# A graph network on one core: in the attention's second pass, odd chunks are weighted on POOL and even chunks on DVE

## The chip, the cores and the metric

The kernel runs on one core of a Trainium2 chip. The metric is the device time of one execution in microseconds (us). A core has several engines that run side by side, each with its own in-order list of instructions: PE (TensorE, matrix products into PSUM), DVE (VectorE, elementwise work), ACT (ScalarE, functions), POOL (GpSimd, slower elementwise work and indirect gathers) and SP, which here only issues DMA transfers. They hand work to each other through semaphores: an instruction adds to one when it is done, and another engine waits for a value.

## The reference

Four graph layers run one after the other over the same 3125 nodes (256 features) and 100000 edges, with a layer norm after each. The one that the change touches is the third, an attention over the edges that end in a node:

```
h = (x @ W.T).reshape(n, H, D)                      # H = 8 heads of D = 32
alpha = leaky(einsum(h[src], a_src) + einsum(h[dst], a_dst) + sum(enc * h[dst]))
amax = segment_max(alpha, dst)
ex = exp(alpha - amax[dst])
denom = segment_sum(ex, dst)
attn = ex / max(denom[dst], 1e-10)
out = segment_sum(h[src] * attn[..., None], dst)
return out.reshape(n, H * D) + bias
```

## The kernel before

The edges are sorted by the node in which they end and cut into NCD = 808 chunks of 128 edges, one edge for each of the 128 partitions. The nodes stand in 25 blocks of 128, and a chunk's edges all end in one block. The attention has two passes over the chunks. The first gathers the source rows h[src] (with POOL's indirect DMAs), makes the logits `alpha`, follows their maxima, and writes the gathered rows to `rows_spill` in DRAM. The second pass, which the change touches, turns them into sums. It starts with an all-engine meeting (`meet`), after which DVE carries the maxima from chunk to chunk (`carry_vector`, L1976 to L1997, some 70 us, with small products on PE at L1963), in two halves of 404 chunks; once a half's logits are lowered by their maxima, ACT may take their exponentials.

Then, for each chunk c, five engines work in a chain.

- SP reads the chunk's rows (128 x 256 values, 128 KB) from `rows_spill` into slot c % 16 of `hs` (L1921). It does so once the rows that the slot held, those of chunk c - 16, have been weighted.
- ACT, for each group of four chunks, writes the exponentials for the 8 heads into columns D to TW (256 to 263) of four of the eight slots of `msg` (L1951). It may do so once the chunk that used the last of these slots before has been summed by PE: for group i that is chunk 4i - 5. ACT also makes the one-hot matrices `oh3` that say in which row of its block each edge ends (L1942 and L1944, five instructions a group), seven groups deep.
- DVE multiplies each row by its exponentials, head by head, from `hs` into columns 0 to 255 of slot c % 8 of `msg` (`weighted_rows`, L1928). Both inputs lie in SBUF. It waits for the exponentials, for the rows, and for PE to have summed chunk c - 8.
- PE multiplies the one-hot matrix with the 264 columns of `msg` (L1973) into PSUM bank c % 8. In the profile this is two weight loads and two matmul records a chunk.
- DVE adds the bank to the sums of the chunk's block in `big` (L2012), four chunks behind its multiplication; one input is in PSUM, one in SBUF. The block's number is in a register. Sixteen of them are loaded at once (L82), so once in sixteen chunks. Consecutive chunks often have the same block, so each sum waits for the one before it to be complete (`added`).

Program order on DVE is thus: multiply chunk n, add chunk n - 4, multiply chunk n + 1, add chunk n - 3, and so on. POOL clears `hsrc` at the start of the pass (L1933) and then waits for the meeting that ends it.

The semaphores are used again under other names, and the rows of the program show the first name: `prefix_kept` is `msgs_v` (messages made by DVE), `mids_g` becomes `msgs_g`, `blocks_counted` is `exps`, `lanes_turned` is `accs_zeroed`.

Of the kernel before, what the change touches and what calls it, by code (L numbers as in the profile page):

```python
# [9 lines left out]
def up(n, m):  # L10
    return -(-n // m) * m
# [17 lines left out]
NCD = up((E + (P - 1) * NB) // P, 8)  # L29
GS = 2  # L30
NUS = up((E + (GS * P - 1) * NB) // (GS * P), 16)
# [54 lines left out]
def program(nc, t, out):  # L86
    with ExitStack() as ctx:
        v, a, pe, g, sp = nc.vector, nc.scalar, nc.tensor, nc.gpsimd, nc.sync
        known = {}

        def signal(name):
            if name not in known:
                known[name] = Signal(ctx.enter_context(nc.semaphore(name)))
            return known[name]

        def again(old, count):

            new = Signal(old.s)
            new.over(old.base + count)
            return new  # L100
# [52 lines left out]
        def lanes(col, n, k):  # L153
            return col.rearrange("p (n o) -> p n o", o=1).to_broadcast([col.shape[0], n, k])
# [1162 lines left out]
        mixed, mids_v, mids_g = signal("mixed"), signal("mids_v"), signal("mids_g")  # L1317
# [381 lines left out]
        RB = 16  # L1699
# [214 lines left out]
        carry_used, lowered = again(counted_used, 2), again(counted_hot, 2 * NBATCH)  # L1914
        exps, msgs_v = again(step_done, NBATCH + 1), again(prefix_kept, NBATCH)

        def sums_sync():
            for c in range(NCD):
                if c >= RB:
                    sp.wait_ge(msgs_v.s, msgs_v.n(c - RB + 1))  # L1920
                sp.dma_start(hs[:, c % RB, :], rows_spill[c]).then_inc(spill.s(c, RB), 16)  # L1921

        def weighted_rows(eng, c):
            eng.wait_ge(exps.s, exps.n(c // 4 + 1))
            eng.wait_ge(spill.s(c, RB), spill.n(c, RB))
            if c >= 8:
                eng.wait_ge(summed.s, summed.n(c - 7))
            return eng.tensor_tensor(msg[:, c % 8, 0:D].rearrange("p (h d) -> p h d", h=H),  # L1928
                                     hs[:, c % RB, :].rearrange("p (h d) -> p h d", h=H),
                                     lanes(msg[:, c % 8, D:TW], H, HD), ALU.mult)  # L1930

        def sums_pool():
            g.memset(hsrc, 0.0).then_inc(accs_zeroed.s, 1)  # L1933

        def sums_scalar():
            for n in range(NCD + 6):
                if n < NCD and n % 4 == 0:
                    i, hot = n // 4, oh3[n // 4 % OH3]
                    if i >= OH3:
                        a.wait_ge(summed.s, summed.n(4 * (i - OH3) + 4))  # L1940
                    for k in range(4):
                        ins = a.activation(hot[:, k, :], iota, ACT.Abs, bias=recd3[:, n + k, D_DL:D_DL + 1], scale=-1.0)  # L1942
                    then_a(ins)
                    a.activation(hot, hot, ACT.Relu, bias=1.0, scale=-1.0).then_inc(hot_made.s, 1)  # L1944
                c = n - 6
                if c >= 0 and c % 4 == 3:
                    i = c // 4
                    a.wait_ge(lowered.s, lowered.n(1 if 4 * i + 4 <= CH else 2))
                    if i >= 2:
                        a.wait_ge(summed.s, summed.n(4 * i - 4))  # L1950
                    a.activation(msg[:, 4 * (i % 2):4 * (i % 2) + 4, D:TW], alpha[:, 4 * i:4 * i + 4, :],  # L1951
                                 ACT.Exp).then_inc(exps.s, 1)

        def sums_tensor():
            pe.wait_ge(carried.s, carried.n(1))
            k = 0
            for half in range(2):
                cs = slice(half * CH, (half + 1) * CH)
                for h in range(H):
                    for reach in (fwd, bwd):  # L1960
                        if k >= 8:
                            pe.wait_ge(carry_used.s, carry_used.n(k - 7))
                        pe.matmul(ps[k % 8][:, 0:CH], lanes(ident[0:H, h:h + 1], 1, P)[:, 0, :], reach[:, cs],  # L1963
                                  start=True, stop=True).then_inc(carry_spread.s, 1)
                        k += 1
            pe.wait_ge(carry_used.s, carry_used.n(4 * H))
            pe.wait_ge(accs_zeroed.s, accs_zeroed.n(1))
            for c in range(NCD):
                pe.wait_ge(hot_made.s, hot_made.n(c // 4 + 1))
                pe.wait_ge(msgs_v.s, msgs_v.n(c + 1))  # L1970
                if c >= 8:
                    pe.wait_ge(added.s, added.n(c - 7))
                pe.matmul(ps[c % 8][:, 0:TW], oh3[c // 4 % OH3][:, c % 4, :], msg[:, c % 8, :],  # L1973
                          start=True, stop=True).then_inc(summed.s, 1)
# [24 lines left out]
        def sums_vector():  # L1999
            blk = Numbers(v, regs_v, blk_d_row, NB - 1)  # L2000
            v.wait_ge(accs_zeroed.s, accs_zeroed.n(1))
            for n in range(NCD + 4):
                c = n
                if c < NCD:
                    weighted_rows(v, c).then_inc(msgs_v.s, 1)
                c = n - 4
                if c >= 0:
                    v.wait_ge(summed.s, summed.n(c + 1))
                    if c >= 1:
                        v.wait_ge(added.s, added.n(c))  # L2010
                    here = big[:, bass.ds(blk.at(c) * TW, TW)]
                    v.tensor_tensor(here, here, ps[c % 8][:, 0:TW], ALU.add).then_inc(added.s, 1)  # L2012
            v.wait_ge(added.s, added.n(NCD))

        sums_sync()
        sums_pool()
        sums_scalar()
        sums_tensor()
        carry_vector()
        sums_vector()  # L2020
        summed.over(NCD)
        added.over(NCD)
# [134 lines left out]
```

## Time and profile before

| | |
|---|---|
| median of 3 runs | 10667.19 us |
| lowest, highest | 10627.23, 10682.18 us |
| the profiled execution | 10687.69 us |
| its span | 10685.9 us |
| second pass, first weighted row to last sum | 8720.1 to 9329.3 us |
| DVE, PE, ACT busy in 8720 to 9330 | 553.07, 545.84, 400.20 us |
| POOL busy in 8720 to 9330 | 0.00 us |

The span runs from the first instruction to the last. A timeline row gives the start, the duration, the engine, the line and the operands, and in square brackets how long the engine had been idle and what released it. On DVE, instructions overlap a little: a multiplication is recorded with 0.42 us, but the next instruction may start 0.34 us after it. So what a sequence costs is read from the starts, not from the durations.

### The profile page before, as it was taken

Reading aid. Unit: us, or ns where it says so; the run is one execution under the profiler, and the core shown is the slowest. Engines: PE = TensorE matmul, PEld = TensorE weight load, DVE = VectorE, ACT = ScalarE, POOL = GpSimd, SP = SyncE. Lnnn points to the kernel's source line nnn. Section 1 sums busy time; section 2 is a strip of 40 time slices with the busy share of each in tenths; the row PEclk is TensorE's granted clock in tenths of the full one; section 3 lists DMA queues with packets and bytes.
Section 4 is the critical chain, followed back from the end, with each engine's and each line's share of the span. In section 5 each row is a group of like instructions: output and inputs, shape, how many; then the busy total and the mean of one; then the engine's idle time right before and its main releaser. Section 6 shows DMA issues by size and latency. Waiting matters only on the chain. (4 is left out here: it accounts for less than half of the span.)

```text
span 10685.9 us, 108870 instructions
## 1 busy us (share of the span) xinstructions
PE 6312.3 (59%) x23693; PEld 3434.3 (32%) x23693; DVE 5953.1 (56%) x17820; ACT 2842.7 (27%) x9327; POOL 5768.1 (54%) x6086
## 2 busy tenths in 40 slices
PE   2211344446865666666667777765555578856665
PEld 1101233334433333433334111233333333333332
DVE  8915533430016666544445999976656589943333
ACT  0000000105862222100003777762222236500000
POOL 5776566561006666566662888844555510046664
PEclk9999855558987877888887999996666679978877
DMA  2000111113553333433332555534666645523333
GB/s 79 6 6 5 36 42 46 44 33 124 176 194 96 93 93 93 109 91 91 91 90 67 168 171 169 171 91 141 189 184 186 185 128 176 153 80 91 92 91 82
DMA packets 782920, 1136.72 MB, mean 106 GB/s; under 512 B 161213, under 2 KB 631923, under 8 KB 775629
## 3 DMA queue, kind: packets, MB, share of 16 engines
q0 software_dynamic: 246400, 552.44, 19.6%
q1 hardware_dynamic: 535885, 577.31, 16.6%
q8 instruction: 216, 3.54, 0.1%
q14 instruction: 419, 3.43, 0.1%
HBM read 872.21 MB, written 257.00 MB: 106 GB/s over the span
## 5 line engine op out<-in xcount | busy, mean ns | idle before, releaser
L1155 POOL DMA_INDIRECT ring<-scaled_table,idx_s x832 | 787.2, 946 | 1181.1 <-DVEq L192 773.7
L1029 POOL DMA_INDIRECT big<-x_table,rec_d_sb x808 | 806.1, 998 | 1101.1 <-DMA x_table<-big 726.0
L1748 POOL DMA_INDIRECT ring<-att_table,rec_d_sb x808 | 775.6, 960 | 750.7 <-DVE acc L1858 287.6
L1427 PE MATMUL bank<-ring,wts 128*128 128x512 f32 x1664 | 937.6, 648 | 397.2 <-issue 166.7
L1105 PE MATMUL bank<-iota 128*128 128x512 bf16 x2448 | 1090.0, 445 | 0.0
L333 POOL DMA_INDIRECT rec_s<-acc,big x784 | 837.6, 1068 | 375.0 <-issue 253.7
L1349 POOL DMA_INDIRECT ring<-y_table,idx_s x832 | 815.2, 980 | 395.5 <-DVEq L192 171.3
L333 POOL DMA_INDIRECT rec_d<-x_res,big x784 | 750.5, 957 | 502.0 <-DVE big L596 255.5
L1155 POOL DMA_INDIRECT ring<-h_table,rec_d_sb x808 | 764.1, 946 | 470.6 <-issue 180.4
L1116 PE MATMUL bank<-big,ring 128*128 128x256 f32 x1616 | 620.5, 473 | 501.0 <-issue 363.7
L2088 PE MATMUL bank<-ring 128*128 128x256 f32 x1664 | 644.9, 475 | 421.0 <-DVE ring L2070 244.4
L1182 PE MATMUL bank<-ring 128*128 128x256 f32 x1616 | 634.5, 480 | 387.0 <-issue 354.8
L1370 ACT ACTIVATE ring<-ring,big 128x64 f32<-128x64 f32 x2496 | 680.3, 335 | 269.1 <-DVE ring L1392 171.8
L1767 PE MATMUL bank<-big 128*128 x2424 | 622.8, 388 | 198.7 <-issue 129.6
L1174 DVE TENSOR_TENSOR acc<-acc,bank 128x256 f32 x808 | 340.4, 421 | 622.6 <-PE bank L1182 257.1
L400 ACT COPY big<-bank 128x425 f32<-128x425 f32 x49 | 25.2, 514 | 2195.6 <-PE bank L455 1613.6
L1116 PEld LDWEIGHTS bank<-big,ring 128*128 128x128 f32 x1616 | 375.7, 242 | 718.6 <-issue 640.1
L1427 PEld LDWEIGHTS bank<-ring,wts 128*128 128x128 f32 x1664 | 253.8, 191 | 1080.4 <-issue 472.6
L1973 PE MATMUL bank<-ring 128*128 128x264 f32 x1616 | 545.8, 425 | 78.5 <-issue 58.6
L1855 DVE TENSOR_TENSOR ring<-bank,wts 128x256 f32<-128x256 f32 x808 | 337.6, 418 | 440.9 <-ACT wts L1809 257.1
L2088 PEld LDWEIGHTS bank<-ring 128*128 128x128 f32 x1664 | 328.7, 223 | 761.9 <-DVE ring L2070 434.4
L1809 ACT ACTIVATE wts<-bank 128x256 f32<-128x256 f32 x808 | 302.1, 383 | 998.5 <-remote 453.6
(344 smaller groups left out, 13324.4 us busy)
## 6 DMA issues: line engine op xcount, KB each, us to landing
weights_dram<-acc SPq DMA_DIRECT2D x104, 1024.0 KB, 4.5
ring<-weights_dram SPq DMA_DIRECT2D x832, 128.0 KB
rows_spill<-ring SPq DMA_DIRECT2D x808, 128.0 KB
big<-rows_spill SPq DMA_DIRECT2D x808, 128.0 KB, 2.2
ring<-key_dram SPq DMA_DIRECT2D x49, 1024.0 KB
big<-dl_dram SPq DMA_DIRECT2D x50, 512.0 KB
ring<-y_table,idx_s POOLq DMA_INDIRECT x832
ring<-scaled_table,idx_s POOLq DMA_INDIRECT x832
```

The costliest lines, as they stand in the source:

```text
L333: g.indirect_dma_start(out=table, out_offset=bass.IndirectOffsetOnAxis(ap=row_of[k][:, j:j + 1], axis=0), in_=stage[:, j, :], in_offset=No ...
L1029: g.indirect_dma_start(out=xg[:, c % RG, :], out_offset=None, in_=x_table, in_offset=bass.IndirectOffsetOnAxis(ap=recd3i[:, c, D_IDX:D_IDX ...
L1105: pe.matmul(ps[7].rearrange("p (o k) -> p o k", o=2), iota[:, 0:P // 2].bitcast(BF16), spare, start=True, stop=True)
L1116: pe.matmul(ps[c % 7][:, 0:D], onehot[:, c % 8, :], xg[:, c % RG, 0:D], start=True, stop=True).then_inc(summed.s, 1)
L1155: g.indirect_dma_start(out=slot[:, c % ring_len, :], out_offset=None, in_=table, in_offset=bass.IndirectOffsetOnAxis(ap=index(c), axis=0)) ...
L1182: pe.matmul(ps[c % 7][:, 0:D], hot4[:, c % 4, :], hg[:, c % R2, :], start=True, stop=True).then_inc(summed.s, 1)
L1349: g.indirect_dma_start(out=yg[:, n % RY, MUL:], out_offset=None, in_=y_table, in_offset=bass.IndirectOffsetOnAxis(ap=idx_s[:, n:n + 1], ax ...
L1370: ins = a.mul(dots[:, c % 2, d * MUL:(d + 1) * MUL], y[:, (1 + d) * MUL:(2 + d) * MUL], recs3[:, c, S_SH + 1 + d:S_SH + 2 + d])
L1427: pe.matmul(ps[6 + u % 2], oh1[c // 4 % 2][:, c % 4, :], mid[:, c % 2, 0:512], start=(c % GS == 0), stop=(c % GS == GS - 1)).then_inc(summ ...
L1748: g.indirect_dma_start(out=ag[:, n % R3, :], out_offset=None, in_=att_table, in_offset=bass.IndirectOffsetOnAxis(ap=recd3i[:, n, D_IDX:D_I ...
L1767: ins = pe.matmul(ps[c % 3][:, 0:TW], hot_n[:, i % 3, k * P:(k + 1) * P], big_b[:, bass.ds(at + s * TW, TW)], start=(s == 0), stop=(s == 2))
L2088: pe.matmul(ps[3 + u % 4][:, 0:D], oh4[:, c % 4, :], sg[:, c % R4, :], start=(c % GS == 0), stop=(c % GS == GS - 1)).then_inc(summed.s, 1)
```

## The change

POOL multiplies the rows of the odd chunks, 404 of the 808, in a list of its own after it has cleared `hsrc`; DVE multiplies those of the even chunks. The function is the same, with another engine. The messages are counted by two semaphores, one for each engine, and those who wait for a message (PE, before the product, and SP, before it reads new rows into the slot) wait for the one that belongs to the chunk. DVE still adds every chunk, at the same place.

```diff
+        msgs_g = again(mids_g, NUS)
+
+        def message_made(eng, c):
+
+            made_by = msgs_g if c % 2 else msgs_v
+            eng.wait_ge(made_by.s, made_by.n(c // 2 + 1))
+
         def sums_sync():
             for c in range(NCD):
                 if c >= RB:
-                    sp.wait_ge(msgs_v.s, msgs_v.n(c - RB + 1))
+                    message_made(sp, c - RB)
...
         def sums_pool():
             g.memset(hsrc, 0.0).then_inc(accs_zeroed.s, 1)
+            for c in range(1, NCD, 2):
+                weighted_rows(g, c).then_inc(msgs_g.s, 1)
...
-                pe.wait_ge(msgs_v.s, msgs_v.n(c + 1))
+                message_made(pe, c)
...
-                if c < NCD:
+                if c < NCD and c % 2 == 0:
                     weighted_rows(v, c).then_inc(msgs_v.s, 1)
```

On DVE, this stands in a row before, from the multiplication of chunk 8 to that of chunk 11 (L1928 multiplies, L83 sets the register with the block's place, L2012 adds):

```order
L1928 TENSOR_TENSOR ring<-big,ring 128x256 [waits summed,spill8,blocks_counted]
L83 ISA [waits added,summed]
L2012 TENSOR_TENSOR big<-big,bank4 128x264
L1928 TENSOR_TENSOR ring<-big,ring 128x256 [waits summed,spill9,blocks_counted]
L83 ISA [waits added,summed]
L2012 TENSOR_TENSOR big<-big,bank5 128x264
L1928 TENSOR_TENSOR ring<-big,ring 128x256 [waits summed,spill10,blocks_counted]
L83 ISA [waits added,summed]
L2012 TENSOR_TENSOR big<-big,bank6 128x264
L1928 TENSOR_TENSOR ring<-big,ring 128x256 [waits summed,spill11,blocks_counted]
```

And with the change, from the same chunk 8 on (L1935 multiplies, L2021 adds):

```order
L1935 TENSOR_TENSOR ring<-big,ring 128x256 [waits summed,spill8,blocks_counted]
L83 ISA [waits added,summed]
L2021 TENSOR_TENSOR big<-big,bank4 128x264
L83 ISA [waits added,summed]
L2021 TENSOR_TENSOR big<-big,bank5 128x264
L1935 TENSOR_TENSOR ring<-big,ring 128x256 [waits summed,spill10,blocks_counted]
L83 ISA [waits added,summed]
L2021 TENSOR_TENSOR big<-big,bank6 128x264
L83 ISA [waits added,summed]
L2021 TENSOR_TENSOR big<-big,bank7 128x264
L1935 TENSOR_TENSOR ring<-big,ring 128x256 [waits summed,spill12,blocks_counted]
```

Every second addition now follows directly on the one before it. On POOL, the odd chunks' multiplications follow the clearing of `hsrc`:

```order
L1940 MEMSET big 128x6600 [waits engines_met]
L1935 TENSOR_TENSOR ring<-big,ring 128x256 [waits spill1,blocks_counted]
L1935 TENSOR_TENSOR ring<-big,ring 128x256 [waits spill3,blocks_counted]
L1935 TENSOR_TENSOR ring<-big,ring 128x256 [waits spill5,blocks_counted]
L1935 TENSOR_TENSOR ring<-big,ring 128x256 [waits spill7,blocks_counted]
L1935 TENSOR_TENSOR ring<-big,ring 128x256 [waits summed,spill9,blocks_counted]
L1935 TENSOR_TENSOR ring<-big,ring 128x256 [waits summed,spill11,blocks_counted]
```

Before, nothing stood behind the MEMSET on this engine until the meeting; now 404 multiplications do, each of which waits for its exponentials, its rows and, from chunk 9 on, for PE.

## Rows read from the trace of the kernel before

**Rows 1.** Busy time by stretch: start:end, length, engines, clock share, DMA, GB/s
```profile
8646.00:8720.00 74.00, 46.33 (x64) 19.73 (x64) 69.64 (x72) 10.88 (x31) 5.60 (x1) 0.50 0.09 29
8720.00:9330.00 610.00, 545.84 (x1616) 242.54 (x1616) 553.07 (x1619) 400.20 (x1185) 0.00 (x0) 1.00 0.58 171
```

**Rows 2.** Timeline, DVE in the pass: start, duration, engine, line [idle before]
```profile
8998.23 0.42 DVE L1928 TENSOR_TENSOR ring<-big,ring 128x256 f32<-128x256 f32 x1
8999.66 0.43 DVE L2012 TENSOR_TENSOR big<-big,bank 128x264 f32 x1 [1.01 <-PE bank L1973]
9000.00 0.42 DVE L1928 TENSOR_TENSOR ring<-big,ring 128x256 f32<-128x256 f32 x1
9000.34 0.42 DVE L2012 TENSOR_TENSOR big<-big,bank 128x264 f32 x1
...
9011.57 0.43 DVE L2012 TENSOR_TENSOR big<-big,bank 128x264 f32 x1 [1.02 <-PE bank L1973]
```

**Rows 3.** Timeline, DVE at the pass's end, where additions follow additions
```profile
9326.32 0.42 DVE L2012 TENSOR_TENSOR big<-big,bank 128x264 f32 x1
9326.96 0.43 DVE L2012 TENSOR_TENSOR big<-big,bank 128x264 f32 x1 [0.22 <-DVE big L2012]
9327.61 0.43 DVE L2012 TENSOR_TENSOR big<-big,bank 128x264 f32 x1 [0.22 <-DVE big L2012]
```

**Rows 4.** Timeline, all engines at the pass's start
```profile
8720.11 1.76 DVE L1928 TENSOR_TENSOR ring<-big,ring 128x256 f32<-128x256 f32 x5
8720.67 3.42 PE L1973 MATMUL bank<-ring 128*128 128x264 f32 x7 [17.78 <-DVE ring L1928]
8723.18 0.43 DVE L2012 TENSOR_TENSOR big<-big,bank 128x264 f32 x1 [1.31 <-PE bank L1973]
```

**Rows 5.** Busy time by stretch, as rows 1: start of the pass; a later product
```profile
8720.60:8724.10 3.50, 3.42 (x8) 2.73 (x9) 2.19 (x7) 0.00 (x0) 0.00 (x0) 0.50 0.64 185
9410.30:9413.00 2.70, 2.70 (x14) 2.10 (x12) 2.27 (x6) 0.37 (x1) 0.00 (x0) 1.00 0.00 0
```

**Rows 6.** Timeline, PE in that later product
```profile
9410.31 2.75 PE L913 MATMUL bank<-wts,ring 128*128 128x256 f32 x12
```

**Rows 7.** Timeline, from chunk 19's multiplication to ACT's next exponentials
```profile
8732.98 0.41 DVE L1928 TENSOR_TENSOR ring<-big,ring 128x256 f32<-128x256 f32 x1
...
8733.46 0.30 PEld L1973 LDWEIGHTS bank<-ring 128*128 128x128 f32 x2 [0.38 <-issue]
...
8734.27 0.23 ACT L1951 ACTIVATE ring<-acc 128x32 f32<-128x32 f32 x1 [0.64 <-PE bank L1973]
...
8734.41 1.26 ACT L1942 ACTIVATE ring<-iota,rec_d_sb 128x128 f32<-128x128 f32 x4
8735.70 0.63 ACT L1944 ACTIVATE ring<-ring 128x512 f32<-128x512 f32 x1
```

**Rows 8.** Second layer, L1341 and its instructions: duration ns min/median/max, first and last start
```profile
L1341 POOL TENSOR_TENSOR ring<-ring,big x416: 507/517/694, 5808.1 to 7102.9; 128x192 f32<-128x192 f32 x139
```

**Rows 9.** Timeline, second layer, POOL and DVE, POOL released by DVE
```profile
6213.61 0.28 DVE L1400 TENSOR_TENSOR ring<-ring 128x128 f32<-128x128 f32 x1
...
6213.97 0.51 POOL L1341 TENSOR_TENSOR ring<-ring,big 128x192 f32<-128x192 f32 x1 [0.63 <-DVE ring L1400]
```

**Rows 10.** Timeline, second layer, POOL and DVE at once, inputs in SBUF
```profile
6501.59 0.36 DVE L1397 TENSOR_TENSOR ring<-ring 128x192 f32<-128x192 f32 x1 [0.18 <-PE bank L1427]
6501.63 0.68 POOL L1341 TENSOR_TENSOR ring<-ring,big 128x192 f32<-128x192 f32 x1
...
6501.86 0.60 DVE L1400 TENSOR_TENSOR ring<-ring 128x128 f32<-128x128 f32 x1
```

**Rows 11.** Timeline, second layer, POOL beside an addition from PSUM
```profile
6142.90 0.52 POOL L1341 TENSOR_TENSOR ring<-ring,big 128x192 f32<-128x192 f32 x1
6142.93 0.68 DVE L1414 TENSOR_TENSOR acc<-acc,bank 128x512 f32 x1
```

**Rows 12.** L1414 and its instructions in the whole second layer
```profile
L1414 DVE TENSOR_TENSOR acc<-acc,bank x416: 672/674/689, 5813.6 to 7104.8; 128x512 f32 x139
```

## The prediction

> **What bounds the kernel now.** I read the busy times by stretch first. In the second pass (8720 to 9330) DVE is busy 553 us of 610 and PE 546, while POOL has nothing and PE has its full clock, 1.00 [rows 1]. Busy time doesn't say which of DVE and PE is the bound, since both overlap their own instructions. The timeline of DVE does. A multiplication starts 0.34 us after an addition and an addition 0.34 us after a multiplication: 8999.66, 9000.00, 9000.34 [rows 2]. That is about 0.675 us for a chunk without a gap, and PE follows at that pace: its weight load starts 0.48 us after the multiplication [rows 7]. PE could go faster. Its records of 256 columns in a product without waits take 2.75 us for 12, 0.23 each, at clock 1.00 [rows 5, 6], so 0.24 for 264 columns and 0.47 for a chunk of two. ACT has five instructions and the exponentials in a group of four chunks, from 8734.27 to about 8736.33, 2.1 us out of 2.7 [rows 7]. So DVE is the bound.
>
> DVE also has a hole every sixteen chunks, when it loads block numbers: 8998.23 to 8999.66 is 1.43 us where 0.34 is usual, 1.09 too much, and the next such addition comes 11.91 us after this one [rows 2]. The name of PE in that row is misleading: PE is up to date there, and the distance is just that of L82's load of sixteen numbers. 11.91 is 16 times 0.676 and 1.09.
>
> **What leaves DVE, and what comes to light.** 404 multiplications leave it. At 0.34 us each that would be 136 us. But an addition must wait for the one before it, and the rows at the end of the pass show what that costs where nothing is between: 9326.32, 9326.96, 9327.61, a start every 0.65 us, with DVE idle 0.22 us and released by L2012 itself [rows 3]. Before, the multiplication filled just this hole: addition to addition with it takes 9000.34 less 8999.66, 0.68 us [rows 2]. Taking it out gives 0.65 in place of 0.675, and that is all. For two chunks DVE now has multiplication, addition, addition: 0.337 + 0.65 + 0.337 = 1.325 us in place of 1.35. The gain is 0.025 us for each of 404 pairs, 10.1 us. The load of the numbers stays, at the same place behind a multiplication of an even chunk.
>
> At the start, five multiplications stand before the first addition, 1.76 us in all [rows 4]; three stand there now, which is 0.7 us less, or nothing if PE, which runs at clock 0.50 there, 0.49 us a record [rows 4, 5], is late with its first sums. I take 0.7.
>
> **What POOL costs itself.** No row shows a 128 x 256 multiplication on POOL. The nearest is the same operation with 192 columns and a broadcast input, 517 ns [rows 8]. The bounds are 0.52 us (no dependence on the width) and 0.69 us (in proportion, 517 x 256 / 192). I take 0.66, nearer to the upper one, because 0.52 us for 192 columns must be mostly per element. POOL needs one in 1.325 us, so it is half idle at either bound, and its list has nothing else until the meeting. It starts within 0.08 us of its releaser: L1400 ends at 6213.89, POOL starts at 6213.97 [rows 9]. SP and PE wait for the same messages as before through another semaphore; I cost this at nothing, as POOL's come earlier than DVE's did.
>
> **Where POOL and DVE meet.** In the second layer a POOL multiplication that started at 6501.63 took 0.68 us instead of 0.52, behind a DVE multiplication that had started at 6501.59; and the DVE multiplication issued at 6501.86 took 0.60 us, where the same one takes 0.28 [rows 9, 10]. DVE thus worked from 6502.18 to 6502.46, and stood until 0.13 us before POOL's end. The two exclude one another while POOL reads: 0.52 less 0.13 is 0.39 us for 192 columns, and 0.66 less 0.13 is 0.53 us for 256. An addition with one input in PSUM isn't held: beside POOL from 6142.93 on it took 0.68 us [rows 11], and its median is 674 ns [rows 12]. So the 808 additions are free of it, the 404 multiplications left on DVE are not.
>
> The Trainium skill, "SBUF — State Buffer", section "Who interferes with whom", says that a DVE instruction with two SBUF inputs contends with a POOL instruction that reads SBUF, that the one that started first has the shared pair for its whole instruction and the other fully blocks, and that one SBUF input doesn't contend. The trace agrees, except that DVE was let in 0.13 us before POOL's recorded end. By the page's words alone the hold would be 0.66 instead of 0.53 us, which would put the hold's end below at 2.73 and cost 16 us in place of my 4.
>
> Does the hold fall on a multiplication? POOL's two instructions of a group both wait for the same exponentials, since the PE sum that frees their slots also frees ACT's. So they come as a pair each 2.65 us. Count from the start of the multiplication of chunk 4i-6 on DVE: PE starts after 0.48; it does that chunk and then chunk 4i-5, whose message is ready, 0.47 later; from a chunk's weight load to the exponentials it releases are 8734.27 less 8733.46, 0.81; exponentials 0.23; POOL 0.08 [rows 7, 9]. The sum is 2.07. POOL's first instruction then holds until 2.07 + 0.53 = 2.60. DVE's multiplications start at 1.325, 2.65 and 3.975. The one at 2.65 gets in by 0.05 us; POOL's second waits behind it until about 2.9 and holds until some 3.5, clear of 3.975. With 0.69 for POOL and 0.50 for PE's chunk the hold ends at 2.66, about 2 us over the 202 groups; with some tenths more it is slower in proportion, because DVE then waits in every group for a loop that starts with its own multiplication. I take 4 us, bounds 0 and 20, the latter for a loop that is 0.1 us longer.
>
> At the start, POOL's first four multiplications run during the carry stage, where the exponentials of the first half are ready; each can hold DVE by up to 0.53 us, 0 to 2.1. I take 1.
>
> **Sum.** -10.1 - 0.7 + 4 + 1 = -5.8 us. From the profiled execution's 10687.7 us that gives 10681.9. It stands 20.5 us above the median of the runs shown (10667.2), so on the median the forecast is 10661 us: no change that can be told, since a measurement of this kernel tells about 0.5%, 53 us.
>
> **Rivals.**
>
> Held multiplications (slower). If the loop is longer than I counted, POOL's first instruction of each pair takes hold just before DVE's multiplication. The most it can cost is the whole hold, 0.53 us in each of 202 groups, 107 us; if POOL's second also wins against the next multiplication, 404 x 0.53, 214 us. It decides by when POOL starts relative to 2.65: at 2.12 or before nothing is lost, from there on the loss grows by 0.1 us a group for each 0.1 us, and for a start past 2.65 DVE is first. For a result over 0.5% it needs 65 us of holds, 0.32 us a group, a loop of 2.97 instead of 2.65. For it: my margin is 0.05 us and four links were added up. Against it: 0.3 us is more than any one link seems off by. Typical time: 10667 - 11 + 107 = 10763. Chance 12%. Milder holds, 20 to 50 us net, stay within 0.5%; they have some 15% of the forecast's 81.
>
> The gain as meant (faster). If the 0.65 us between additions were not the wait for the one before but something that the multiplication on DVE costs too, all 0.337 x 404 = 136 us would go, down to 10531; PE's 0.47 and ACT's 2.1/4 a chunk would allow it. Rows 3 speak against it: there is no other work there, and the profile itself names L2012 as the releaser. 3%, with 2% for a median that scatter puts 0.5% lower.
>
> POOL as bound, or PE's clock lost (slower). POOL would need over 1.325 us for what takes 0.52 to 0.69, and PE's work is the same in slightly less time, so its clock of 1.00 has no reason to fall. At clock 0.50 a chunk costs 0.98 us [rows 4] against 11.91/16 = 0.744 [rows 2], 190 us more, 10857. 2%.
>
> **How the numbers follow.** No change to tell 81%, slower 14% (12 and 2), faster 5%. The likeliest case gives 10661. Its own scatter is that of the runs shown, 40 us down and 15 up from the median, and the milder holds add up to 50. The range 10620 to 10720 takes these in and leaves out the two far rivals.
>
> **What would show it.** In the changed kernel's timeline DVE should show multiplication, addition, addition with starts at 0.34, 0.65 and 0.34 us, and idle 0.22 before each odd addition, released by L2021. The pass should take about 600 us instead of 610, with DVE busy near 0.42 x 404 us less. POOL should show 404 instructions of 0.6 to 0.7 us, in pairs each 2.65 us, the second of a pair some 0.2 longer. Multiplications of 0.42 us on DVE mean that none is held; if every second one takes 0.6 to 0.9, the held rival is right, and the pass is longer than before. Additions closer than 0.6 us to one another would break the argument.

## The result, and the profile after

| | before | changed |
|---|---|---|
| median, 22 runs each | 10637.76 us | 10679.28 us |
| ratio, 95% interval | | 1.0036 [1.0018, 1.0053] |
| profiled execution's span | 10685.9 us | 10703.4 us |
| second pass, first row weighted by DVE to last sum | 8720.1 to 9329.3, 609.2 us | 8694.4 to 9354.3, 659.9 us |
| DVE's 404 multiplications of even chunks, mean | 416 ns | 572 ns |

The changed kernel is slower by 0.36%, 19 to 56 us. That is within the 0.5% that I had called no change, but it is clear of zero, and on the other side of the 6 us gain that I forecast. The spans of the two profiled executions hide most of it: the second pass began 26 us earlier in the changed one, in stages whose code is the same. The pass itself is 50.7 us longer, within the interval of the whole.

Three groups of the changed kernel in the pass; the columns are line, engine, operation, operands, count, then busy us and mean ns, then idle time before them and what ended it:

```profile
L2021 DVE TENSOR_TENSOR big<-big,bank 128x264 f32 x808 | 343.9, 426 | 145.6 <-DVE big L2021 87.1 <-PE bank L1982 57.6 <-issue 1.0
...
L1935 POOL TENSOR_TENSOR ring<-big,ring 128x256 f32<-128x256 f32 x400 | 238.6, 618 | 442.4 <-ACT ring L1960 442.4
L1935 DVE TENSOR_TENSOR ring<-big,ring 128x256 f32<-128x256 f32 x404 | 230.7, 572 | 0.4
```

The first line shows the hole that was to come to light: 87.1 us in which an addition waits for the one before it. Before, it was filled by multiplications, and such waits came to 0.9 us, as the same line of the kernel before shows:

```profile
L2012 DVE TENSOR_TENSOR big<-big,bank 128x264 f32 x808 | 339.6, 420 | 56.3 <-PE bank L1973 55.1 <-DVE big L2012 0.9 <-issue 0.3
```

The second line has 400 of POOL's 404 multiplications; the first four ran in the carry stage. The third line is the surprise: DVE's multiplications take 572 ns on average. At 0.418 us each, the duration of one that isn't held, 404 would take 169 us; they took 231. The 62 us more are what the pass lost, against 10 us won.

DVE at the start of the pass, in the timeline:

```profile
8711.97 0.42 DVE L1935 TENSOR_TENSOR ring<-big,ring 128x256 f32<-128x256 f32 x1
8712.30 0.42 DVE L2021 TENSOR_TENSOR big<-big,bank 128x264 f32 x1
8712.95 0.43 DVE L2021 TENSOR_TENSOR big<-big,bank 128x264 f32 x1 [0.22 <-DVE big L2021]
8713.29 0.87 DVE L1935 TENSOR_TENSOR ring<-big,ring 128x256 f32<-128x256 f32 x1
8714.08 0.42 DVE L2021 TENSOR_TENSOR big<-big,bank 128x264 f32 x1
```

The starts 0.33, 0.65, 0.34 are the forecast ones [rows 2, 3]. Then a multiplication takes 0.87 us and all behind it comes 0.45 later. In the pass 129 of the 404 take about 0.87 us and 19 something between; all but one of these 148 are of chunks 4i - 2, every second one of DVE's. And here is a whole turn of the loop, with POOL (x2 is its pair of multiplications in one row):

```profile
9003.82 0.54 DVE L1935 TENSOR_TENSOR ring<-big,ring 128x256 f32<-128x256 f32 x1
...
9005.27 0.42 DVE L1935 TENSOR_TENSOR ring<-big,ring 128x256 f32<-128x256 f32 x1
...
9005.69 0.23 ACT L1960 ACTIVATE ring<-acc 128x32 f32<-128x32 f32 x1 [1.04 <-PE bank L1982]
...
9006.00 1.19 POOL L1935 TENSOR_TENSOR ring<-big,ring 128x256 f32<-128x256 f32 x2 [1.91 <-ACT ring L1960]
...
9006.60 0.87 DVE L1935 TENSOR_TENSOR ring<-big,ring 128x256 f32<-128x256 f32 x1
```

The first multiplication was itself held 0.12 us, so count from 9003.94. The exponentials come 1.75 us later (worked out before: 1.76), POOL's pair 2.06 later (2.07). The row merges POOL's pair. A narrower window, 9006.70 to 9007.10, has its second multiplication by itself:

```profile
9006.57 0.62 POOL L1935 TENSOR_TENSOR ring<-big,ring 128x256 f32<-128x256 f32 x1
```

It starts 0.57 us behind the first, at 2.63. DVE's multiplication comes at 2.66, 0.03 us too late. It finds POOL reading, works from 9007.05 to 9007.47, and so is let in 0.14 us before POOL's end at 9007.19; in rows 10 that was 0.13. From 9003.94 to 9007.05 the group took 3.11 us instead of 2.65. The next pair of POOL is released by this very multiplication, so it comes with the same distance again: in each of the 129, POOL's second starts 0.02 to 0.03 us ahead of DVE's multiplication. The kernel is locked into the bad rhythm. Only the load of block numbers, once in four groups, puts DVE behind and lets one group pass: there DVE's multiplication comes at 3.76, and POOL's second has ended at 3.24. Three held groups in four are 3 x 0.45 = 1.35 us in sixteen chunks. With eight pairs of 1.325 and the load's 1.09 that makes 13.04 us, and 13.07 is what sixteen chunks take, from the addition behind one load to that behind the next:

```profile
8722.70 0.43 DVE L2021 TENSOR_TENSOR big<-big,bank 128x264 f32 x1 [1.02 <-PE bank L1982]
...
8735.77 0.43 DVE L2021 TENSOR_TENSOR big<-big,bank 128x264 f32 x1 [1.02 <-PE bank L1982]
```

### The profile page after: what moved, and what is told of

Read it like the earlier page. It is cut to its first block and busy times, and to the rows that moved or that the text cites. A ratio compares the mean times of both kernels' runs of the same rounds, so it can differ in the third digit from the quotient of the medians.

```text
span 10703.4 us, 108870 instructions
## 1 busy us (share of the span) xinstructions
PE 6268.1 (59%) x23693; PEld 3489.7 (33%) x23693; DVE 5910.9 (55%) x17416; ACT 2841.3 (27%) x9327; POOL 6009.4 (56%) x6490
## 5 line engine op out<-in xcount | busy, mean ns | idle before, releaser
L1155 POOL DMA_INDIRECT ring<-scaled_table,idx_s x832 | 786.7, 946 | 504.4 <-PE bank L2097 167.2
L333 POOL DMA_INDIRECT rec_s<-acc,big x784 | 836.5, 1067 | 357.3 <-issue 253.8
L333 POOL DMA_INDIRECT rec_d<-x_res,big x784 | 750.6, 957 | 508.6 <-DVE big L596 260.4
L1155 POOL DMA_INDIRECT ring<-h_table,rec_d_sb x808 | 763.9, 945 | 458.8 <-issue 178.6
L1982 PE MATMUL bank<-ring 128*128 128x264 f32 x1616 | 457.9, 407 | 216.8 <-issue 134.9
```

What stands on the lines that cost most here:

```text
L333: g.indirect_dma_start(out=table, out_offset=bass.IndirectOffsetOnAxis(ap=row_of[k][:, j:j + 1], axis=0), in_=stage[:, j, :], in_offset=No ...
L1155: g.indirect_dma_start(out=slot[:, c % ring_len, :], out_offset=None, in_=table, in_offset=bass.IndirectOffsetOnAxis(ap=index(c), axis=0)) ...
```

## The experiments

Two theories stood against each other from the start. A: DVE is held while POOL reads, and it is the phase that decides (A1: POOL's second multiplication takes hold just ahead of DVE's). Rivals: DVE isn't held, the loop through PE and ACT is longer (B); a reading POOL costs DVE the same wherever it stands (A2); DVE without multiplications would be far faster (C, E); with more work on POOL, the loop through POOL, ACT and PE becomes the bound (D). The pass's length tells them apart far better than the whole time, which scatters by 50 us and more. It is 609.2 us before and 659.9 with the change. "Held time" is the sum of what DVE's multiplications take above 0.418 us each, 62.1 us with the change. All diffs are against the changed kernel.

**POOL writes but doesn't read.**

```diff
...
             for c in range(1, NCD, 2):
-                weighted_rows(g, c).then_inc(msgs_g.s, 1)
+                if c >= 3:
+                    g.wait_ge(waited.s, c // 2)
+                g.wait_ge(exps.s, exps.n(c // 4 + 1))
+                g.wait_ge(spill.s(c, RB), spill.n(c, RB))
+                if c >= 8:
+                    g.wait_ge(summed.s, summed.n(c - 7))
+                g.memset(idle_columns, 0.0).then_inc(waited.s, 1)
+                g.memset(msg[:, c % 8, 0:D], 0.0).then_inc(msgs_g.s, 1)
```

> Leaves out the weighting of the odd chunks: POOL writes zeros into their messages and into 384 spare columns (two MEMSETs, about as long as a multiplication), at the same waits, but reads nothing. Theory A (DVE's multiplications are held while POOL reads SBUF): no multiplication of DVE over 0.43 us; the pass (first weighted row to last sum; 609.2 us before, 659.9 with the change) falls to about 599 us. Rival B (the pass is longer because PE and ACT now wait for POOL's messages in their loop, not because DVE is held): POOL is as busy and is waited for as before, so the pass stays at about 660 us.

Measured: pass 598.7 us, and DVE's 404 multiplications take 416 ns at least and 426 at most. In the timeline POOL writes from 9002.02 on, and DVE multiplies at 9002.23 as if alone:

```profile
9002.02 0.31 POOL L1951 MEMSET ring<- 128x256 f32 x1
9002.23 0.42 DVE L1935 TENSOR_TENSOR ring<-big,ring 128x256 f32<-128x256 f32 x1
```

151 of the 404 begin while a MEMSET of POOL runs, and none is held. B falls: messages at the same waits, with a POOL somewhat busier (292 us in the pass, 239 with the change), cost nothing. What costs is that POOL reads SBUF while DVE wants two inputs from it.

**No weighting of odd chunks at all.**

```diff
+            if c % 2 and (c >= 8 or eng is sp):
+                eng.wait_ge(spill.s(c, RB), spill.n(c, RB))
+                eng.wait_ge(exps.s, exps.n(c // 4 + 1))
+                return
...
-                weighted_rows(g, c).then_inc(msgs_g.s, 1)
+                if c < 8:
+                    g.memset(msg[:, c % 8, 0:D], 0.0).then_inc(msgs_g.s, 1)
```

> Leaves out the weighting of the odd chunks altogether: no POOL instruction after the first four, DVE multiplies the even chunks and adds all. This is the most that taking 404 multiplications off DVE can bring. Theory A with additions that wait for one another (0.65 us apart): pass about 598 us, 11 us less than the 609.2 before. Rival C (a DVE without the multiplications would run at 0.34 us for each of them less, and POOL takes that back): pass about 475 to 500 us.

Measured: pass 598.7 us, as with a POOL that only writes. So the most that taking 404 multiplications off DVE can bring is 10.5 us, not 136. The hole between dependent additions takes the rest. C falls.

**POOL's second multiplication goes behind DVE's.**

```diff
             for c in range(1, NCD, 2):
+                if c % 4 == 3 and c >= 7:
+                    g.wait_ge(msgs_v.s, msgs_v.n((c - 5) // 2 + 1))
                 weighted_rows(g, c).then_inc(msgs_g.s, 1)
```

> The change, with one wait more: POOL's second multiplication of a group (chunk 4i+3) waits until DVE has multiplied chunk 4i-2, so it can't take hold just ahead of it. Theory A1 (it is POOL's second that catches DVE: POOL's pair starts 2.06 us after the multiplication that releases it and the second 0.58 us later, at 2.64, while DVE's multiplication is due at 2.65): the multiplications of 0.87 us are gone, held time falls from 62 us to under 10, pass 598 to 605 us. Rival A2 (a POOL that reads holds DVE for about as long per instruction wherever it stands): held time stays at about 60 us, pass about 660 us.

Measured: pass 599.1 us; two multiplications of the 404 are held, by 0.16 us each, where 148 were. POOL does the same work with the same reads, one wait later:

```profile
9004.67 0.62 POOL L1935 TENSOR_TENSOR ring<-big,ring 128x256 f32<-128x256 f32 x1 [0.94 <-ACT ring L1962]
...
9005.26 0.42 DVE L1935 TENSOR_TENSOR ring<-big,ring 128x256 f32<-128x256 f32 x1
...
9005.76 0.62 POOL L1935 TENSOR_TENSOR ring<-big,ring 128x256 f32<-128x256 f32 x1 [0.48 <-DVE ring L1935]
```

DVE slips in between the two, at 9005.26, just before POOL's first ends by the record, at 9005.29, and POOL's second now stands behind it. A1 holds and A2 falls: 61 us hang on one wait.

**POOL does more, later.**

```diff
...
+                if c % 4 == 1:
+                    g.wait_ge(exps.s, exps.n(c // 4 + 1))
+                    g.memset(idle_columns, 0.0).then_inc(waited.s, 1)
+                    g.wait_ge(waited.s, c // 4 + 1)
                 weighted_rows(g, c).then_inc(msgs_g.s, 1)
```

> The change, with one more small MEMSET of 8 spare columns on POOL before each pair, and a wait for it: POOL does more and its pair starts some 0.2 us later. Theory A1: POOL's first now holds until about 2.26 + 0.48 = 2.74, so DVE's multiplication due at 2.65 waits 0.1 us but then comes before POOL's second; a group takes 2.75 to 2.8 us instead of 3.10 and the pass is shorter, 610 to 630 us. Rival A2: more work on POOL, pass 660 us or more.

Measured: pass 609.5 us, 50 less than the change and just under the 610 to 630 expected, with 202 instructions more on POOL. The timeline shows the turn that was expected:

```profile
9003.82 0.10 POOL L1946 MEMSET ring<- 128x8 f32 x1 [1.14 <-ACT ring L1966]
...
9004.00 1.37 POOL L1935 TENSOR_TENSOR ring<-big,ring 128x256 f32<-128x256 f32 x2
...
9004.43 0.47 DVE L1935 TENSOR_TENSOR ring<-big,ring 128x256 f32<-128x256 f32 x1
```

DVE now asks while POOL's first still reads, waits 0.05 us, and is in before the second, which waits in its turn: the pair takes 1.37 us instead of 1.19. 145 multiplications are held, nearly as many as with the change (148), but for 11.2 us in all, not 62. Only three of them take over 0.8 us.

**The change again, timed with two versions beside it.** These three and the next ran in a later session, in which all kernels took 15% less time (see the last section).

> The changed kernel as it is, again. Theory A1: the locked rhythm isn't chance, so the pass shows it again: 655 to 665 us, held time near 62 us, and the whole is 0.2 to 0.6% slower than before. If the rhythm depended on how this one execution happened to start, the held time would come out elsewhere, 20 or 90 us.

Measured: pass 660.1 us, 129 multiplications of about 0.87 us, held time 62.5 us: the locked rhythm is the kernel's own. The whole is 1.0061 [1.0036, 1.0086] of before. The medians, 9096.87 and 9017.69 us, lie further apart than this ratio, by 0.9%; the pass accounts for 51 us, 0.56%.

The version with the wait, same diff as above:

> The change with POOL's second multiplication of a group waiting for DVE's multiplication of chunk 4i-2, timed. Pass 599 us, 10 us less than before and 61 less than with the change: 0.1% faster than before, which is within what can't be told, ratio 0.997 to 1.001; against the change alone 0.4 to 0.6% faster.

Measured: pass 599.3 us, the whole 0.9996 [0.9971, 1.0021] of before. The loss is gone; a gain of 10 us can't be told from none. Against the change the medians (9027.04 and 9096.87 us) are 70 us apart, 0.8%, where 0.4 to 0.6% was expected. The pass shows 61 of these. For the other 9 no interval is on record; single runs of one kernel lie up to 78 us apart.

**POOL weights everything.**

```diff
-            made_by = msgs_g if c % 2 else msgs_v
-            eng.wait_ge(made_by.s, made_by.n(c // 2 + 1))
+            eng.wait_ge(msgs_g.s, msgs_g.n(c + 1))
...
-            for c in range(1, NCD, 2):
+            for c in range(NCD):
                 weighted_rows(g, c).then_inc(msgs_g.s, 1)
...
-                if c < NCD and c % 2 == 0:
-                    weighted_rows(v, c).then_inc(msgs_v.s, 1)
```

> POOL weights all 808 chunks, DVE only adds. Theory A1 with dependent additions 0.65 us apart: nothing on DVE reads two SBUF inputs, so nothing is held; POOL needs 0.59 us a chunk and keeps ahead; per 16 chunks DVE takes 16 x 0.65 + 1.09 = 11.49 us, pass about 583 us, 26 less than before, ratio about 0.9975. Rival A2 (a reading POOL slows whatever DVE does): additions beside POOL take over 0.43 us, pass over 610 us. Rival D (POOL, ACT and PE in one loop become the bound): additions wait for PE, over 0.65 us apart, pass 600 us or more.

Measured: from first to last addition 586.3 us, where before takes 606.1 (8723.2 to 9329.3) and the change 656.8. That is 20 us less than before; 26 had been expected. The whole is 0.9965 [0.9942, 0.9989] of before, 8985.34 us against 9017.69: faster than both kernels. POOL's multiplications and DVE's additions, with duration ns min/median/max and first and last start:

```profile
L1934 POOL TENSOR_TENSOR ring<-big,ring x808: 609/615/1212, 7143.7 to 7754.3; 128x256 f32<-128x256 f32 x162
```

```profile
L2018 DVE TENSOR_TENSOR big<-big,bank x808: 424/430/431, 7176.9 to 7762.8; 128x264 f32 x162
```

No addition takes over 431 ns, though POOL reads for most of the time: an addition with one input in PSUM isn't held. 589 of the 808 begin while POOL reads. 745 additions start 0.65 us behind the one before, and 11.53 us lie between two loads (7502.34 to 7513.87), where 11.49 was worked out. D falls too, since these additions don't wait for PE. Twelve others start 1.0 us behind the one before, which makes 4 of the 6 us that are missing: the kernel before has twelve of these too, and the working had left them out. What holds them up, no run here shows.

**POOL weights one chunk in four.**

```diff
-            made_by = msgs_g if c % 2 else msgs_v
-            eng.wait_ge(made_by.s, made_by.n(c // 2 + 1))
+            if c % 4 == 3:
+                eng.wait_ge(msgs_g.s, msgs_g.n(c // 4 + 1))
+            else:
+                eng.wait_ge(msgs_v.s, msgs_v.n(c - c // 4 + 1))
...
-            for c in range(1, NCD, 2):
+            for c in range(3, NCD, 4):
...
-                if c < NCD and c % 2 == 0:
+                if c < NCD and c % 4 != 3:
```

> POOL weights chunk 4i+3 only, DVE the three others. Theory A1, by the same working as for the change: count from the multiplication of chunk 4i-6. POOL's releaser comes at 2.06, but DVE's multiplication of chunk 4i-3 began at 2.0 and reads until 2.27, so POOL holds from 2.27 to 2.75, and the multiplication due at 2.675 waits 0.1 us: a group takes about 2.75 us, held time 10 to 20 us, pass about 612 to 620 us. Rival A2 (holds in proportion to POOL's instructions): held time 31 us, half of the change's, pass about 635 us. Rival E (DVE is freed of a quarter and gains 0.34 x 202 = 68 us): pass 540 us.

Measured: pass 617.7 us, held time 14.7 us. Here both engines wait in turn:

```profile
7500.35 0.42 DVE L1937 TENSOR_TENSOR ring<-big,ring 128x256 f32<-128x256 f32 x1
7500.40 0.84 POOL L1937 TENSOR_TENSOR ring<-big,ring 128x256 f32<-128x256 f32 x1 [1.92 <-ACT ring L1962]
...
7501.02 0.50 DVE L1937 TENSOR_TENSOR ring<-big,ring 128x256 f32<-128x256 f32 x1
```

POOL waits 0.22 us for DVE's reads, and then DVE 0.08 for POOL's. The pass is longer than before (609.2) with a quarter of DVE's multiplications gone, as the phases say and E doesn't.

## Why the prediction was wrong

**The bound and what comes to light: right.** DVE was the bound, additions in a row start every 0.65 us, and the gain of the freed multiplications is 10.5 us (pass 598.7 against 609.2) where the sum had 10.1 and 0.7. The 0.7 at the start was nothing, as allowed for: from the first multiplication to the first addition it is 3.07 us in both kernels. Who reads only how much DVE is freed of, 136 us, is wrong by a factor of 13.

**The carry stage: 1 us taken, 0.1 measured.** It took 73.9 us before (8646.2 to 8720.1) and 74.0 after (8620.4 to 8694.4).

**The place where POOL and DVE meet: this step failed.** The links were right to 0.01 us: exponentials at 1.75, POOL at 2.06. So was the hold: until 0.14 us before POOL's end. What failed was "The one at 2.65 gets in by 0.05 us; POOL's second waits behind it". I had asked when POOL's first lets go, and never worked out when the second starts. With the 0.66 us that I took for a multiplication on POOL it would start at about 2.07 + 0.62 = 2.69 (in the trace the two rows of a pair overlap by 0.04), behind DVE. But it takes 0.615; that 0.52 us for 192 columns "must be mostly per element" did not hold (see the last section). With that the first lets go at 2.06 + 0.48 = 2.54, with even more room; the second starts at 2.62 or 2.63, ahead of DVE's 2.65 or 2.66, and it is this one that holds. By this working a POOL that was faster than assumed made the kernel slower. No run has a slower multiplication on POOL; the one in which the pair only comes later has 11.2 us of held time in place of 62. The term that I put at 4 us, bounds 0 and 20, measured 62 (two sums of the trace agree: the durations above 0.418 in the rows, and 659.9 less 598.7, 61.2). The upper bound moved only one number, the length of the loop, and kept the order of events. My own lower bound for POOL, 0.52 us, would have shown the trap: by the same working the second starts at 2.55 and holds until 2.94, 0.29 us in each of 202 groups, an estimate of 59 us. The bound should have taken the whole hold wherever two events were 0.05 us apart.

**The rivals.** The right one was "Held multiplications", at 12%. Its mechanism, its place and the most it can cost per group (0.53; 0.45 measured) stand. Its case against, that 0.3 us is more than any link is off by, was beside the point, since being off by 0.05 in the duration was enough when a second instruction follows. What it priced as a smooth growth of 0.1 us for 0.1 us has a step in it: a start 0.03 us earlier or later decides about 0.45 us. Its typical time had all 202 groups held; three in four are. The net loss in the pass, 50.7 us, is just past the milder holds of 20 to 50 us net, to which I had given some 15% inside the forecast's 81. The sign named for this rival came: 147 of the 202 multiplications of chunks 4i - 2 are held and the pass is longer than before. The chances by outcome were not upset, since 0.36% lies within 0.5%, and the median of 10679 us lies in my range. Neither speaks for the mechanism: the range was made wide by the scatter of whole runs, and it would have held a gain of 6 us as well as this loss. The sign was wrong, and the likeliest case should not have had 81%.

**What DVE and POOL share.** The Trainium skill, "SBUF — State Buffer", "Who interferes with whom", says that the one that starts first has the pair for its whole instruction, and that a POOL instruction that only writes isn't in the way of a DVE instruction with two SBUF inputs. The experiments bear out the second: 0.42 us beside a writing POOL, up to 0.87 beside a reading one. They bear out the first but for its end: the measured hold ends 0.14 us before POOL's recorded end. They also agree with what the prediction took from there on one SBUF input: none of 808 additions is held beside a reading POOL.

## What to carry to other kernels

Before an engine is relieved, look at what its remaining instructions wait for when they stand next to each other: here a multiplication of 0.34 us filled a hole of 0.31, and moving it away was worth 0.025. Before POOL is given elementwise work beside DVE, write down which DVE instructions read two SBUF inputs, and when POOL's start relative to them; if one event of a loop releases the other, a difference of 0.03 us decides about every turn, and a wait on POOL, or giving POOL all of the two-input work, settles it. A margin smaller than the error of its terms is no margin: price the case on its other side in full.

## What the runs showed of the hardware that I had not expected

POOL's multiplication of 256 columns took 0.615 us where one of 192 took 0.517: 1.5 ns for a column more. If the two differ in nothing but the width, more than 0.2 us of it don't depend on the width, which is an estimate from these two. In proportion it would have been 0.69.

In the later session all kernels took 9.0 ms instead of 10.7, while the second pass, which has no indirect transfers, was the same to 0.2 us (659.9 and 660.1). The gathers on POOL show a part of the difference, here those of one stage (L1155). One of them takes 946 ns by its record in both sessions, but 808 of them take 1168 us in the kernel before, of the first session (4441.1 to 5609.4), and 1013 in the changed one, of the later session (3361.1 to 4373.6; the code is the same at this line): 1.45 and 1.25 us apiece.

The largest part, some 665 of the 1600 us, is another one. A stage in which PE and ACT make weights for the edges (L834) came behind POOL's first indirect transfers (L333) in the first session, from 2449.7 to 3121.3 in the changed kernel, and beside them in the later, from 1345.0 to 2036.6. From the last of L333 to POOL's next indirect transfer it was 720 us in the one (2455 to 3175) and 55 in the other (2174 to 2230). Why, for both parts, no run here shows. It is why the pass's length was compared, and ratios only within a session.
